# Splitting T and Q in PSUM instead of in an SBUF staging tile (cross attention, 16 batches, fp32)

## The reference

```
g_x     = _conv1x1(g_w, g_b, x_2).transpose(0, 2, 1)
theta_x = _conv1x1(theta_w, theta_b, x).transpose(0, 2, 1)
phi_x   = _conv1x1(phi_w, phi_b, x_2)
W  = jnp.einsum('bnc,bcm->bnm', theta_x, phi_x) / phi_x.shape[-1]
y  = jnp.einsum('bnm,bmc->bnc', W, g_x).transpose(0, 2, 1)
wy = _conv1x1(w_w, w_b, y)
wy = bn_gamma * (wy - bn_mean) * rsqrt(bn_var + EPS) + bn_beta
return wy + x
```

## Time and profile before

| | us |
|---|---|
| median of the three runs | 801.82 |
| the profiled execution | 801.54 |
| its span, first to last instruction | 799.8 |
| TensorE matmuls busy | 779.1 |
| VectorE busy | 532.4 |
| GpSimd busy | 538.7 |
| ScalarE busy | 304.2 |

### The profile page before, as it was taken

How to read it: one execution, slowest core, us unless ns; L and a number is a source line. 1 busy time by engine, 2 the same in 40 slices (tenths; PEclk the granted TensorE clock), 3 DMA queues, 4 the chain that set the end, 5 groups by cost and what they waited for, 6 DMA issues and landing times.

```text
span 799.8 us, 11592 instructions
## 1 busy us (share of the span) xinstructions
PE 779.1 (97%) x4045; PEld 666.2 (83%) x4045; DVE 532.4 (67%) x892; ACT 304.2 (38%) x512; POOL 538.7 (67%) x357
## 2 busy tenths in 40 slices
PE   5889999999999999999999999999999999999997
PEld 4578888888888888888888888888888888888886
DVE  5967583965848577584866748487584866758254
ACT  3633341435424253441435334243452425334131
POOL 5949675785857688575786857588585777857500
PEclk9989999999999999999999999999999999999999
DMA  9816437072551717346082642707355072630202
GB/s 279 177 78 161 155 74 242 1 211 105 126 190 40 228 47 184 131 86 229 1 212 102 154 161 53 246 15 190 125 103 211 23 210 82 157 158 1 106 1 105
DMA packets 55127, 103.17 MB, mean 129 GB/s; under 512 B 2474, under 2 KB 37956, under 8 KB 55108
## 3 DMA queue, kind: packets, MB, share of 16 engines
q1 hardware_dynamic: 52976, 101.86, 43.2%
q10 hardware_dynamic: 2132, 1.05, 0.6%
HBM read 69.35 MB, written 33.55 MB: 129 GB/s over the span
## 4 chain that ended last, share of the span: by engine, by line
PE 96%; issue 1%; DMA 1%; POOL 1%; DVE 0%; ACTq 0%; ACT 0%; DVEq 0%; POOLq 0%
PE wbank L664 57%; PE gbank L664 36%; PE wbank L827 1%; PE wbank L706 1%; DMA vec_rows<-in_L_xattn_g_b_dram 1%; POOL ctxT_lo L286 0%; PE wbank L683 0%; PE wbank L712 0%; POOL ctx_sum L297 0%; ACTq L144 0%; ACTq L138 0%; DVE low_lo L579 0%; PE wbank L695 0%; DVE junk L595 0%; DVE x_sb L654 0%
## 5 line engine op out<-in xcount | busy, mean ns | idle before, releaser
L286 POOL TENSOR_TENSOR ctxT_lo<-ctxT,ctxT_hi 128x512 fp32r<-128x512 f32 x124 | 167.8, 1354 | 207.6 <-ACT ctxT_hi L340 207.6
L297 POOL TENSOR_TENSOR ctx_sum<-ctx_sum,ctxT 128x512 f32<-128x512 f32 x108 | 163.8, 1517 | 0.2
L315 POOL TENSOR_TENSOR x_lo<-x_sb,x_hi 128x1024 fp32r<-128x1024 f32 x60 | 142.4, 2406 | 0.0
L340 ACT ACTIVATE mt<-wbank 128x512 fp32r<-128x512 f32 x64 | 37.9, 598 | 245.0 <-PE wbank L664 245.0
L654 DVE SCALAR_TENSOR_TENSOR x_sb<-wbank,const,x_sb 128x512 f32<-128x512 f32 x112 | 79.0, 747 | 67.6 <-PE wbank L664 67.6
L664 PE MATMUL wbank<-ctxT_lo,ctxT_hi 128*128 128x512 f32 x512 | 121.8, 394 | 0.0
L521 DVE TENSOR_TENSOR stage<-gbank,mt 128x384 f32<-128x384 f32 x64 | 28.4, 486 | 139.7 <-PE gbank L664 139.7
L340 ACT ACTIVATE ctxT_hi<-ctxT 128x512 fp32r<-128x512 f32 x124 | 76.7, 628 | 92.2 <-DVE ctxT L479 92.1
L664 PEld LDWEIGHTS wbank<-ctxT_lo,ctxT_hi 128*128 128x128 f32 x512 | 95.6, 190 | 18.6
L664 PE MATMUL wbank<-x_hi,wt_hi 128*128 128x512 f32 x256 | 82.6, 404 | 5.7 <-issue 5.7
L479 DVE STREAM_TRANSPOSE ctxT<-ctx_sb 128x512 f32<-128x512 f32 x124 | 79.0, 683 | 7.5 <-DMA ctx_sb<-in_ctx_dram 7.4
(11 more groups left out here) (107 smaller groups left out, 1366.6 us busy)
## 6 DMA issues: line engine op xcount, KB each, us to landing
x_sb<-in_x_dram SPq DMA_DIRECT2D x16, 2048.0 KB, 7.8
out_dram<-x_sb SPq DMA_DIRECT2D x64, 512.0 KB, 2.6
ctx_sb<-in_ctx_dram SPq DMA_DIRECT2D x60, 512.0 KB, 8.4
ctx_sb<-in_ctx_dram ACTq DMA_DIRECT2D x4, 256.0 KB, 5.8
ctx_sb<-in_ctx_dram SPq DMA_DIRECT2D x4, 256.0 KB, 5.8
x_sb<-in_L_xattn_w_w_dram SPq DMA_DIRECT2D x1, 512.0 KB, 9.5
stage<-in_L_xattn_theta_w_dram SPq DMA_DIRECT2D x1, 512.0 KB, 10.4
phi_nat<-in_L_xattn_phi_w_dram SPq DMA_DIRECT2D x1, 512.0 KB, 11.1
```

Of the source, the lines that this page charges most:

```text
L286: nc.gpsimd.tensor_tensor(ctxT_lo[:, c, :], turned_ctx(b, c), f(ctxT_hi[:, c, :]), ALU.subtract).then_inc(sem_, 1)
L297: nc.gpsimd.tensor_tensor(ctx_sum[:, :], ctx_sum[:, :], src, ALU.add).then_inc(ctxT_used, 1)
L315: nc.gpsimd.tensor_tensor(x_lo[:, k, :], x_sb[par][:, k, :], f(x_hi[:, k, :]), ALU.subtract).then_inc(x_lo_made, 1)
L340: nc.scalar.activation(dst, src, ACT.Copy).then_inc(sem_, 1)
```

## The change

T and Q with their bias term are written back to the bank that they came from; ScalarE rounds them from there and VectorE subtracts from there. T block 3 takes the same bank as block 0, so TensorE waits for t_lo of block 0 before it, and no longer for the sum alone. Before Q it waits for the third t_lo (its banks 1 and 2 must be free), then for the fourth at the fourth row block. The wait for the fourth `t_taken` ahead of the outputs goes.

```diff
                 for r, m in enumerate(T_ORDER):
                     act.wait_ge(t_taken, KC * b + (r + 1))
-                    hi(t_hi[:, m, :], stage[:, r * CI:(r + 1) * CI], t_hi_made)
+                    hi(t_hi[:, m, :], gbank[T_BANK[r]][:, 0:CI], t_hi_made)
...
                     act.wait_ge(q_taken, KI * b + (k + 1))
-                    hi(q_hi[:, k, :], stage[:, k * C:(k + 1) * C], q_hi_made)
+                    hi(q_hi[:, k, :], gbank[Q_BANK[k]][:, :], q_hi_made)
...
                     dve.wait_ge(t_hi_made, KC * b + (r + 1))
-                    nc.vector.tensor_tensor(t_lo[:, m, :], stage[:, r * CI:(r + 1) * CI], f(t_hi[:, m, :]),
+                    nc.vector.tensor_tensor(t_lo[:, m, :], gbank[T_BANK[r]][:, 0:CI], f(t_hi[:, m, :]),
                                             ALU.subtract).then_inc(t_lo_made, 1)
...
                     dve.wait_ge(t_done, KC * b + (r + 1))
-                    nc.vector.scalar_tensor_tensor(out=stage[:, r * CI:(r + 1) * CI], in0=bp_row[:, :],
+                    nc.vector.scalar_tensor_tensor(out=gbank[T_BANK[r]][:, 0:CI], in0=bp_row[:, :],
                                                    scalar=s_col[:, m:m + 1],
                                                    in1=gbank[T_BANK[r]][:, 0:CI],
                                                    op0=ALU.mult, op1=ALU.add).then_inc(t_taken, 1)
...
-                    nc.vector.tensor_tensor(q_lo[:, k, :], stage[:, k * C:(k + 1) * C], f(q_hi[:, k, :]),
+                    nc.vector.tensor_tensor(q_lo[:, k, :], gbank[Q_BANK[k]][:, :], f(q_hi[:, k, :]),
...
-                    nc.vector.scalar_tensor_tensor(out=stage[:, k * C:(k + 1) * C], in0=zb_row[:, :],
+                    nc.vector.scalar_tensor_tensor(out=gbank[Q_BANK[k]][:, :], in0=zb_row[:, :],
                                                    scalar=p1[:, k:k + 1], in1=gbank[Q_BANK[k]][:, :],
...
                 t_block(2)
-                pe.wait_ge(t_taken, KC * b + 1)
+                pe.wait_ge(t_lo_made, KC * b + 1)
                 t_block(3)
                 theta(1, (0, 1))
 
-                pe.wait_ge(t_taken, KC * b + 3)
+                pe.wait_ge(t_lo_made, KC * b + 3)
                 for r, j in enumerate(T_ORDER):
-                    pe.wait_ge(t_lo_made, KC * b + (r + 1))
+                    if r == KC - 1:
+                        pe.wait_ge(t_lo_made, KC * b + KC)
...
                 pe.wait_ge(s_taken, b + 1)
-                pe.wait_ge(t_taken, KC * b + 4)
                 out_part(0, 0)
```

## The result

The changed kernel takes 806.24 us (median of 11 runs) against 802.16 for the kernel before (11 runs beside it): a ratio of 1.0044, 95% interval 1.0032 to 1.0056. It is slower by 0.44%, where the prediction had 0.46% and a time of 805.5. The ratio is worked out from all the runs kept, so it isn't quite that of the two medians; one run of the eleven (871 us, at a granted clock of 0.85) is left out of it.

A forecast was written before the change was run, and what follows sets the result against it. TensorE was taken as the bound (busy 779.1 of 799.8 us). 8.5 lost less 4.8 gained gives +3.7 on 801.54, or 805.3; with the runs' median 0.3 higher, forecast 805.5 us, 8-in-10 range 802.8 to 810.5.

The forecast's parts named there:

- the later block 3: T's fourth block waits for t_lo(0) before reusing bank 0: 0.54 us late per steady batch, 8.5 us lost in all.
- the gaps that close: Two late starts of output matmuls per batch, 0.17 us each, vanish: 14 x 0.34 = 4.8 us gained.
- the granted clock: TensorE's clock might fall behind batch 0's longer idle time (1.75 to 2.6 us): a loss named but not counted.
- Each about 0.8 us before TensorE wants it: At the output matmuls, q_lo(0) and the last th_lo would be ready about 0.8 us early.
- with q_lo at 0.68, q_lo(0) ends near 354.1: Before the first output matmul, q_lo shortened to 0.68 us by its PSUM source ends q_lo(0) near 354.1, not 354.98.
- In-place sums: VectorE's bias sums writing into the bank they read: no extra taken; upper bound +0.27 us for T, +0.54 for Q.
- The source of a subtraction: t_lo takes 0.41 us from PSUM against 0.42 from SBUF: no penalty; the skill page's 65 ns would add 1.0 us.
- the sum: Whole kernel: 8.5 us lost less 4.8 gained, +3.7 us on the profiled execution's 801.54.
- The gaps stay: Output-matmul gaps come from the change of operands, so only the block 3 loss remains: 810.3 us, chance 0.10.
- in-place sums are slow: Sums into their own bank double the cost per column, delaying block 3 by 0.77 us: 814.0 us, chance 0.07.
- no wait at block 3: t_lo(0) ends by about 342.6, 0.56 us earlier than worked out; only batch 0 loses: 797.9 us, chance 0.10.
- The cancelling case: t_lo(0) before block 3 comes 0.1 us earlier, so loss and gain nearly cancel: around 803.5 us, chance 0.07.

The follow-up runs named there:

- experiment 4: Changed kernel with T's fourth block in a bank of its own (wbank 1), so it waits for no t_lo: 794.79 us, ratio 0.9906 to the kernel before.
- experiment 5: Changed kernel with theta(1) split around T's fourth block, six matmuls on either side: 795.55 us, ratio 0.9915 to the kernel before.
- experiment 6: Changed kernel with ScalarE's order altered: its copy of the next context's chunk 5 moves behind t_hi(0): 804.08 us, ratio 1.0023 to the kernel before.
- Experiments 1: Changed kernel with only T kept in PSUM, Q going through the staging tile as before: 806.45 us, ratio 1.0046 to the kernel before.
- experiment 8: T in PSUM with its fourth block in wbank 1, Q through the staging tile: 794.69 us, ratio 0.9917 to the kernel before.
- experiment 2: Kernel before with only Q kept in PSUM, T going through the staging tile: 795.60 us, ratio 0.9918 to the kernel before.
- experiment 7: Kernel before, T and Q still staged, with only T's fourth block moved to wbank 1: 801.84 us, ratio 0.9994 to the kernel before.
- experiment 3: Changed kernel with all twelve matmuls of theta(1)'s first half ahead of T's fourth block and its wait: 813.59 us, ratio 1.0140 to the kernel before.

## Why the prediction was right, and where it was off

**The forecast held**: direction, size (0.44% against 0.46%), the later block 3, and the gaps that close, though for these it named only one of two causes. The closeness of the total is in part luck (see the granted clock). Point by point:

- *The later block 3.* Worked out 0.54 us per steady batch, 0.60 in batches 1 and 14, 0.86 in batch 0, nothing in 15. The starts show 0.554, 0.61, 0.88 and 0: 8.75 in all against 8.5. The batch period, forecast at about 47.9, is 47.83. Experiments 4 and 5 remove it with the rest unchanged, experiment 6 shows ScalarE's share.
- *The two gaps.* They closed, but the term was mis-sized: 4.8 predicted, 6.0 found, 0.40 a batch and more in batches 1 and 14. I had counted the two late spacings at each place and not that the ten matmuls between the places were each up to 9 ns slow as well, nor that batches 1 and 14 had a larger second gap. "Each about 0.8 us before TensorE wants it" came out as 1.02 for q_lo(0) and 0.61 for the last th_lo.
- *Their cause* was half right. The step "with q_lo at 0.68, q_lo(0) ends near 354.1" names Q's source as what closes them. Experiments 1 and 8 show that T's source does it as well, by way of GpSimd's place in its list: q_lo(0) then starts near the end of a GpSimd operation and not 1 us before it. The two halves of the change gain the same 6 us, and it is had once. That went unseen in the prediction, since with both halves in, it makes no difference.
- *In-place sums.* Taken at no extra: right, 8 or 9 ns, inside the 0.17 us that lay free.
- *The source of a subtraction.* Measured 0.42 from PSUM against 0.42 from SBUF where GpSimd is quiet. The Trainium skill, VectorE: DVE Perf Modes, TRN2 errata, would add 65 ns for the PSUM source (an estimate from its 120 against 58 cycles); no run here shows it. The prediction says that the page's Rules for kernel authors speak against the change outright; they leave the choice, to accept the PSUM source or to copy first "if you'll do many ops". With the two reads per bank here the copy doesn't pay: the Q half alone is 0.8% faster without it.
- *The granted clock.* The prediction named it as a loss not counted, and it came: 1.3 us in the profiled execution. Without it and the 0.7 us of start-up, the difference of the executions would be 2.8, less than the 3.7 of the sum. The smaller net of stall and gaps and the uncounted clock nearly cancel, so the agreement of the total is better than that of its terms, and that is luck.
- *Rivals.* "The gaps stay" fell with experiment 2, "in-place sums are slow" with the rows of the sums, "no wait at block 3" with its spacing. The mark set for this last one, t_lo(0) done by 342.6, asked for more than was needed: 342.74 would have done, 0.44 us earlier than worked out and not 0.56. The cancelling case didn't come either; block 3 was 0.01 later than worked out, not 0.1 earlier.

Left open: the rule for a subtraction of two SBUF tiles beside GpSimd (experiment 1) fits every t_lo and q_lo in the traces with staging, but no experiment moved GpSimd's list alone. And nothing here shows why the half clock of the start-up lasts longer in one execution than in another.

## What to carry to other kernels

A buffer that is reused inside a stage sets how late its last reader may be: moving work from a copy onto the buffer itself makes that reader two hand-overs later, and on a kernel bound by TensorE that counts in full, while of the 67 us that VectorE saves only the 6 at TensorE's gaps do. Before keeping data in PSUM longer, count the banks and look for one that is idle in that stretch; here that turned +0.44% into -0.94%. When moving work to cover a wait, ask what it was covering where it stood.

## What the runs showed of the hardware that I had not expected

After TensorE's idle time in batch 0, the granted clock fell to its lower level or didn't. The windows behind block 3, one for each kernel: T only in PSUM (2.91 us between the starts), Q only (2.02), theta split (1.58), own bank (0.12):

```profile
57.60:62.70 5.10, 5.05 (x18) 4.57 (x19) 2.68 (x8) 0.77 (x2) 5.10 (x5) 0.50 0.01 3
```

```profile
56.70:60.20 3.50, 3.50 (x15) 3.31 (x16) 3.41 (x5) 1.18 (x3) 3.50 (x4) 0.52 0.02 5
```

```profile
57.80:61.00 3.20, 3.14 (x19) 2.86 (x20) 2.00 (x7) 0.77 (x2) 3.20 (x3) 1.00 0.02 5
```

```profile
55.90:59.00 3.10, 3.10 (x22) 2.84 (x21) 3.00 (x13) 1.99 (x4) 3.10 (x3) 1.00 0.04 8
```

The half clock followed the spacing of 2.9 us in all three profiles that had it (the changed kernel, T only, ScalarE's order), that of 2.0 in one of two (Q only, not the kernel before), and shorter ones never (1.58 in theta split, 1.51 in experiment 7, 1.19 in every batch of experiment 3). It costs 0.09 us for each 256-column matmul and 0.20 for each of 512. What that adds up to depends on how long it lasts: 1.3 us in the changed kernel (2.9 us behind block 3), 2.8 in T only (6.1 us).

The runs of one kernel spread by some 3 us (801.4 to 804.1 before, 804.4 to 808.0 after), those of experiment 4, with no idle time there, by 0.5 (794.5 to 795.0, four runs). The clock behind batch 0 may be the cause, but that isn't shown: each kernel has a single profile, and the run of 801.4 in experiment 8 had no idle time at block 3 either.
